# Writing out 1/std over 512 columns: from GpSimd to a broadcast copy on VectorE

## The reference, cut to what matters

```python
xn = (x - mean(x)) / sqrt(var(x) + 1e-5)            # per row of 512
s = einsum('btd,dm->btm', xn, Win) + bin_            # m = 64
h = relu(s[..., None] * W1 + b1)                     # 16 inner values for each m
g = einsum('btmh,mh->btm', h, W2) + b2
out = x + attention(xn) + einsum('btm,md->btd', g, Wout) + bout
```

## Time and profile before

| | |
|---|---|
| three runs, us | 314.58, 319.86, 320.58 (median 319.86) |
| the profiled execution, from its first to its last instruction | 312.5 us |
| what lies around that span | its own time is not given apart; the fastest run is 2.1 us above the span, the median 7.4 us |
| DVE busy | 259.3 us (83%) |
| POOL busy | 241.0 us (77%) |
| PE busy | 279.0 us (89%) |
| ACT busy | 232.5 us (74%) |
| granted PE clock | 0.997 of full speed |

### The profile page before, as it was taken

The page is one execution under the profiler, slowest core; times in us unless marked ns, Lnnn a source line. Parts: engine busy times, 40 slices in busy tenths (PEclk is TensorE's granted clock), DMA queues, the critical chain, the costliest instruction groups (busy, mean ns, idle before and its releaser), DMA issues.

```text
span 312.5 us, 6071 instructions
## 1 busy us (share of the span) xinstructions
PE 279.0 (89%) x2287; PEld 123.2 (39%) x2287; DVE 259.3 (83%) x400; ACT 232.5 (74%) x282; POOL 241.0 (77%) x209
## 2 busy tenths in 40 slices
PE   4988899889979789899998989898989898989982
PEld 4844645335333353334433343333332434342220
DVE  0759759799799969998889999999998998965544
ACT  1548673758987789859998784879787979797840
POOL 8440999693949959978889793979797979799920
PEclk9999999999999999999999999999999999999998
DMA  7999969988359699798998999699999999551697
GB/s 243 286 367 362 269 181 356 423 211 278 96 172 330 206 271 335 217 356 257 288 266 252 364 289 381 195 339 321 303 351 340 366 354 335 191 229 42 214 339 271
DMA packets 50572, 87.86 MB, mean 281 GB/s; under 512 B 6360, under 2 KB 35184, under 8 KB 46448
## 3 DMA queue, kind: packets, MB, share of 16 engines
q1 hardware_dynamic: 46400, 65.96, 66.6%
q10 hardware_dynamic: 3504, 21.37, 19.6%
q0 software_dynamic: 640, 0.16, 0.8%
HBM read 53.77 MB, written 33.69 MB: 280 GB/s over the span
## 4 chain that ended last, share of the span: by engine, by line
PE 41%; DVE 29%; issue 10%; DMA 8%; ACT 7%; POOL 3%; ACTq 1%; DVEq 0%; POOLq 0%
PE TA L514 10%; PE g L582 10%; DVE stats L1145 8%; DVE x L1118 8%; PE op L619 6%; DMA out_dram<-x 5%; ACT xT L820 3%; DMA b2c<-in_L_ffn_b_dram 3%; PE TA L481 3%; ACT H L845 3%; PE rep L566 2%; PE TA L619 2%; DVE xqT L1128 2%; DVE SL L1139 2%; PE A L328 1%
## 5 line engine op out<-in xcount | busy, mean ns | idle before, releaser
L1272 POOL TENSOR_TENSOR x<-x,bias_row 128x512 f32<-128x512 f32 x128 | 167.7, 1347 | 0.0
L845 ACT ACTIVATE H<-rep,b1c,w1c 128x1024 f32<-128x1024 f32 x124 | 144.4, 1206 | 24.2 <-PE rep L566 21.9
L1145 DVE BATCH_NORM_STATS2 stats<-x 128x6 f32<-128x512 f32 x128 | 78.6, 676 | 8.9 <-DMA x<-in_L_attn_x_dram 8.9
L1118 DVE TENSOR_TENSOR x<-x,op 128x1024 f32<-128x1024 f32 x46 | 55.4, 1204 | 14.7 <-PE op L619 14.5
L582 PE MATMUL g<-H,w2s 128*32 128x512 f32 x512 | 62.6, 599 | 0.4 <-ACT H L845 0.4
L1256 POOL TENSOR_TENSOR rstd<-veps,nhalf 128x8 f32<-128x8 f32 x16 | 26.4, 1648 | 33.5 <-DVE veps L1155 33.3
L619 PE MATMUL op<-wout,G 64*128 64x512 f32 x184 | 49.9, 620 | 1.2 <-ACT G L852 0.8
L514 PE MATMUL TA<-xT,win 128*32 128x512 f32 x208 | 47.0, 593 | 0.3 <-ACT s_full L825 0.3
L514 PE MATMUL TA<-xqT,winq 128*32 128x512 f32 x208 | 47.0, 593 | 0.0
L1128 DVE STREAM_TRANSPOSE xqT<-xq 128x1024 f32<-128x1024 f32 x28 | 34.6, 1236 | 0.8 <-DMA xq<-in_L_attn_x_dram 0.8
L820 ACT ACTIVATE xT<-TA 128x1024 f32<-128x1024 f32 x26 | 26.7, 1025 | 8.2 <-PE TA L481 7.7
(11 more groups left out here) (190 smaller groups left out, 361.9 us busy)
## 6 DMA issues: line engine op xcount, KB each, us to landing
out_dram<-x SPq DMA_DIRECT2D x30, 1024.0 KB, 6.9
x<-in_L_attn_x_dram ACTq DMA_DIRECT2D x10, 2048.0 KB, 11.2
xq<-in_L_attn_x_dram SPq DMA_DIRECT2D x112, 128.0 KB, 7.7
x<-in_L_attn_x_dram SPq DMA_DIRECT2D x12, 1024.0 KB, 10.8
out_dram<-x SPq DMA_DIRECT2D x4, 512.0 KB, 3.3
x<-in_L_attn_Wq_dram SPq DMA_DIRECT2D x1, 1024.0 KB, 17.9
x<-in_L_attn_Wk_dram SPq DMA_DIRECT2D x1, 1024.0 KB, 20.0
x<-in_L_attn_Wv_dram SPq DMA_DIRECT2D x1, 1024.0 KB, 7.7
```

Source lines behind the costliest of these rows:

```text
L845: act.activation(Hr[half][k % len(Hr[half])][:, :], rep_banks(n, half)[:, :], ACT.Relu, bias=b1c[:, half, k:k + 1], scale=w1c[:, half, k:k ...
L1118: dve.tensor_tensor(both, both, sum_banks(n, j)[:, :].rearrange("p (h d) -> p h d", h=2), ALU.add).then_inc(add_done, 1)
L1145: dve.bn_stats(stats[:, j, :], x_sb[m][:, j * D:(j + 1) * D]).then_inc(bn_done, 1)
L1272: pool.tensor_tensor(x_sb[m][:, c], x_sb[m][:, c], bias_row[:, :], ALU.add).then_inc(xc_done, 1)
```

## The change

The copy of `rstd` over 512 columns no longer runs on POOL but on DVE, as a `tensor_copy` with a broadcast source. It has a semaphore of its own, `rwide_done`, on which PE's two transposing steps and POOL's next power wait. In blocks 0 to 2 it stands behind the first rows' statistics of the next block; from block 3 on it stands between `s_low(n-1)` and `add(n-3,2)`.

```diff
+        rwide_done = sem("rwide_done")
...
         def spread_late(n):
-            pe.wait_ge(rstd_done, 2 * n + 2)
+            pe.wait_ge(rwide_done, n + 1)
             pe.wait_ge(ev_done, groups(n + 1))
...
         def spread_rstd(n):
-            pe.wait_ge(rstd_done, 2 * n + 2)
+            pe.wait_ge(rwide_done, n + 1)
...
+        def widen_rstd(n):
+            dve.wait_ge(rstd_done, n + 1)
+            if n > 0:
+                dve.wait_ge(rb_done, n)
+            dve.tensor_copy(rwide[:, :, :, :], rstd[:, :].rearrange("p (b j) -> p j b", b=2).unsqueeze(3)
+                            .to_broadcast([P, TPP // 2, 2, M])).then_inc(rwide_done, 1)
...
                 for j in range(1, early(n + 1)):
+                    if j == 3:
+                        widen_rstd(n)
                     statistics(n + 1, j)
+                if early(n + 1) <= 3:
+                    widen_rstd(n)
...
                 s_low(n - 1)
                 reach(side, n, 5)
+                widen_rstd(n)
                 add(n - 3, 2)
...
         def inv_std(n):
             pool.wait_ge(var_done, n + 1)
             if n > 0:
-                pool.wait_ge(rb_done, n)
+                pool.wait_ge(rwide_done, n)
             pool.tensor_tensor(rstd[:, :], veps[:, :], nhalf[:, 0:TPP], ALU.pow).then_inc(rstd_done, 1)
-            pool.wait_ge(rstd_done, 2 * n + 1)
-            pool.tensor_tensor(rwide[:, :, :, :], rstd[:, :].rearrange("p (b j) -> p j b", b=2).unsqueeze(3)
-                               .to_broadcast([P, TPP // 2, 2, M]),
-                               ones_d[:, :].rearrange("p (b m) -> p b m", b=2).unsqueeze(1).to_broadcast([P, TPP // 2, 2, M]),
-                               ALU.mult).then_inc(rstd_done, 1)
```

## The result

| | before | after |
|---|---|---|
| median of 4 runs, us | 317.22 | 333.47 |
| runs, us | 313.79 to 320.58 | 332.53 to 334.03 |
| span of the profiled execution, us | 312.5 | 332.2 |
| granted clock of PE, mean | 0.997 | 0.964 |
| DVE busy, us | 259.3 | 275.3 |

The changed kernel is slower: the ratio is 1.0616, 95% interval 1.0574 to 1.0658. The forecast was 329.5 with a range of 320 to 337.

What follows compares the result with a forecast made beforehand. DVE was taken as full in plain blocks, with room on POOL. Losses of 4.8 + 4.4 + 4.0 + 0.7 = 13.9 us, less 1.9, gave 12 on the 312.5 us span: 324.5, with surroundings 329.5, range 320 to 337.

Steps and rivals of the forecast that it cites:

- what lies around the span: Outside the profiled span: 2.1 us by the fastest run, 7.4 by the median; forecast taken about midway.
- The copy's price: Plain blocks: copy waits for a POOL add, next `add` starts 1.52 us later, block takes 15.7 us instead of 14.74.
- The first rival: All blocks: the copy never waits for POOL, so only 5 to 7 us are lost; chance 0.14.
- DVE comes last: Plain blocks 10 to 14: DVE is ready for the scaling at 254.98, after PE's product at 254.7, setting the block's end.
- full but for 0.7 us: Plain blocks from block 9 on, before the change: DVE is busy for all but 0.7 us.
- The start: Blocks 0 to 2: copy's place delays PE by 1.8, block 1's wait costs 2.1, block 2 costs 0.9; sum 4.8 us.
- Blocks 3 to 9: Copy costs its wait where POOL adds, its own 0.33 where POOL stands still, little where DVE idles; sum 4.4 us.
- The sum of 4.0 for blocks 10 to 14: Five plain blocks, each 0.8 us longer through the copy's wait for POOL: 4.0 us.
- 0.7 for the end: Block 15, with no statistics behind: only PE's shift is left, 0.7 us.
- The allowance of 1.9 us: Taken off the sum because lateness from the start and blocks 3 and 4 meets DVE's idle time in blocks 5 and 7.
- The 5.3 us between the fastest run and the median: Time put around the span, 2.1 us by the fastest run and 7.4 by the median; the trace does not show what it is.

Runs made afterwards that it cites:

- the held version: The kernel before, with POOL from block 3 on held from its bias adds until DVE has made `SL`: median 315.3 us, ratio 1.0041.
- the start-only run: The kernel before with the change in blocks 0 to 2 alone; POOL writes `rwide` in later blocks: median 322.5 us, ratio 1.0131.

## Why the prediction was right, and where its terms were off

**The number: inside the range, and nearer than its parts.** The forecast for the span was 324.5, the measured one is 332.2, 7.7 too low. To that the forecast added 5.0 us for what lies around the span; in the changed kernel's profiled execution it is 1.8 (334.01 - 332.2), and so it is in the long and short runs of the kernel before (320.88 with a span of 319.1, 314.39 with 312.6). The second error took 3.2 us off the first. That 329.5 lies within 4 us of 333.47 is in part luck; with a rest of 1.8 it would have been 326.3.

**The copy's price: right.** The forecast had the next `add` 1.52 us later behind the subtraction than before. Measured from the subtraction's start it is 1.55 later (2.80 us, 257.79 to 260.59, where it was 1.25), of which 1.43 lie between the copy's start and the `add`. The forecast's 15.7 us for a plain block are 15.6. The copy's mean is 1.12, not near 1.3. The copy is the two-column one: it takes 0.40 us alone, and the maximum in its place, at one column per cycle, 0.67. The Trainium skill, Vector Engine (DVE) Microarchitecture Reference, § 5.1 Performance modes, reports two columns per cycle for one element read 32 times by a one-source operation. This trace agrees, for elements that are read 64 times (0.40 us). The first rival, that the copy never waits, is out: it waits in the blocks where POOL adds, and not where POOL stands still (0.41 to 0.42 in blocks 4 to 6). (Its price was also added up wrong: 312.5 + 2.1 and 5 to 7 us give 319.6 to 321.6, not 318.5.)

**"DVE comes last": right for the changed kernel, most likely wrong for the one before.** Behind the change DVE is idle for 0.1 us of 15.6. But "full but for 0.7 us" was taken as if DVE set the pace, and the held version speaks against it. It made no difference to the forecast's sign, since an added 1.4 us is more than the idle 0.7 either way; it would have misled on a change that takes work from DVE.

**The start: the mechanism right, 4.8 against 6.0.** PE's transpose came at 21.55 (forecast 21.7), and the copy of block 1 waited for the power and then for a POOL add. DVE's step behind that copy, at 32.83 before, came at 37.71: 4.9 us later, where 1.8 + 2.1 = 3.9 were forecast. At least a part of the excess is the clock. It fell behind PE's gap of 2.85 us here and did not behind one of 2.37 in the second execution of the changed kernel, which is 4.6 late at block 3's variance, near the forecast's 4.8. The subtraction in block 1 also took 0.5 us longer than before, in both.

**Blocks 3 to 9: 4.4 against 3.3.** The split was good for blocks 3 and 8, too high for 6 and 9. But the main reason given, the wait for POOL, is not borne out by the sum: with a copy that never waits these blocks lose 3.5 us all the same, and they lose 0.1 with the copy earlier and POOL held.

**The step that failed is one that was left out.** The sum of 4.0 for blocks 10 to 14 and 0.7 for the end counted waits alone at the clock of the kernel before, 0.997. The wait that the change puts on PE, 1.0 to 1.3 us behind the delayed `add`, brings stretches at the lower level, each of which made a block 1.3 us longer; three lie in blocks 10 to 14. There 3.9 us (3 x 1.3) of the measured 7.6 are the clock's, and the other 3.7 are the waits, near the 4.0 of the sum. The end, 2.8 instead of 0.7, goes the same way: with the gaps filled it takes 43.0 us at a clock of 0.97 and 0.99, 0.4 over the kernel before, and 45.4 or 48.2 at 0.90 to 0.93 in the four executions with the copy in this place and the gaps open. Filling the gaps from block 10 on took 5.2 us off the median. In the two executions with the gaps filled no block from 10 to 14 shows a fall, in three of those four others three or four of the five do. That such a gap is no sure cause is shown by the same program once with no fall in its plain blocks and once with four.

**The allowance of 1.9 us** for lateness met by idle time was wrong. What was late at block 3 stayed late: 2.7 us at the start were 2.3 at the end in the start-only run.

**The 5.3 us between the fastest run and the median**, which the forecast put beside the span, lie in the span: long runs have long spans (319.1 us for the run of 320.88). Their cause stays open. The subtraction of block 1 losing the port to a row of POOL adds is the first candidate, since it makes a 5.2 us difference in two executions of one program; the one of block 15 does the like at the end (up to 6.7 us). Two different waits on POOL each left no long run, one of them without guarding the subtraction of block 1.

## What to carry to other kernels

Before an instruction moves from POOL to DVE, look at which DVE instructions of its form (one source in SBUF at two columns per cycle, or two sources in SBUF) end just behind a POOL instruction: such a one costs the rest of POOL's work, here up to 1.1 us on top of 0.40 of its own, and a slower form that waits for nobody can be the better one. If it must go there, put it where POOL stands still, or make POOL wait for it; POOL had the room. An engine with 95% busy time is not yet the bound; a run that gives it time back tells, and a new wait for PE should be priced with the clock, not only with its length.

## What the runs showed that was not expected

- DVE can lose to POOL several times in a row: 6.57 us for a subtraction that takes 0.69 alone, with four more POOL adds let in behind the one under way, while in the plain blocks the same subtraction always got in behind the first add. What decides is not known. The Trainium skill, SBUF — State Buffer, § SBUF: two separate sides, says that whichever starts first holds the shared ports for its whole instruction. The runs agree for the add under way (POOL's add ends at 260.38, the copy that waited for it at 260.66); the row of adds let in ahead of a waiting instruction goes beyond that.
- The same PE gap of 1.0 to 1.3 us was followed by a fall of the clock in some blocks and not in others, in one program (none in five plain blocks, then four in five).
- Two executions of one program can differ by 5.2 us at the start and 2.8 at the end, the first with a subtraction of 6.57 us instead of 1.65 in block 1, the second with one of 3.10 instead of 1.87 or 1.88 in block 15.
- A maximum over an axis of one, at one column per cycle, beat the copy at two by 10 us for the whole kernel.
